# Gathering, adding and normalising both layers' expert results inside the attentions that follow, with all narrow keys and values made in the second routing

## The chip, the cores and the metric

The kernel runs on one core of a Trainium2 chip. The metric is the device time of one execution, in microseconds. Five engines work side by side, each through an instruction list of its own, and meet by semaphores: TensorE (PE), VectorE (DVE), ScalarE (ACT), GpSimd (POOL) and SyncE (SP). SyncE only issues transfers here; GpSimd also issues the indirect ones, which gather or scatter rows by an index tile.

## What is computed

Four layers follow each other on x of 16 batches of 112 tokens, 256 wide, with a context of 375 rows for each batch. Every step is a residual: x = x + f(layernorm(x)). The reference, cut to its last lines and to the two mixtures of experts:

```python
x = x + _L0_xattn_ref(_layernorm(x), ctx, ctx, ...)             # focused linear attention
x = x + _L0_ffn_ref(_layernorm(x), ...)                         # experts, gated
x = x + _L1_xattn_ref(_layernorm(x), ctx, ctx, key_mask, ...)   # tanh attention
x = x + _L1_ffn_ref(_layernorm(x), ...)                         # shared experts
x = x + _L2_xattn_ref(_layernorm(x), ctx, ...)                  # wide softmax, 16 heads of 64
x = x + _L2_ffn_ref(_layernorm(x), ...)                         # experts, normed
x = x + _L3_xattn_ref(_layernorm(x), ctx, ctx, mask, ...)       # narrow softmax, 16 heads of 16
x = x + _L3_ffn_ref(_layernorm(x), ...)                         # ternary

# _L0_ffn_ref, the end: each token takes two expert rows, weighted
ys = yb[jnp.minimum(slot, E * C - 1)] * (weights * kept)[:, None]
out = jnp.zeros((T, D), x.dtype).at[tokens].add(ys)

# _L2_ffn_ref, the end: the same sum, the tokens added, and a layer norm of its own
out = out.reshape(b, s, h) + hidden_states
return _layernorm(out, ln_w, ln_b)
```

## The kernel before

Everything is float32. x stays on the chip as one tile, 112 partitions by 16 batches by 256; nearly every loop runs over the 16 batches. The program is a row of stages, each a block of instruction lists for the five engines; a stage begins when all engines have finished the one before. Inside a stage the lists are written out by hand, and what waits for what is a `wait_ge` on a semaphore; `c.link` and `c.step` (class Chain) make an instruction of VectorE wait for the one before it.

The stages: `focused_attention`, then `routed_experts` for layer 0 (`route`, `run_experts`, `combine`), `tanh_attention`, `shared_experts`, `softmax_attention` wide (L2_xattn), `routed_experts` for layer 2, `softmax_attention` narrow (L3_xattn), `ternary_ffn`. Both layers' expert stages share their code, and the trace drops digits from names: `L_ffnr_`, `L_ffne_` and `L_ffnc_` are route, experts and combine of either layer, `L_xattn_` is either softmax attention.

**route** norms the tokens, computes the experts' logits, picks two for each token, and works out by a running count (`cum`, two matmuls) to which slot each row goes. The weights need an exponential (L2388, ScalarE). GpSimd then issues 32 indirect stores (L2364, 16 batches by 2 choices) that scatter rows to `xbuf` in memory. For layer 2 the stage also prepares the ternary weights of the last stage (`tw.prepare`, `tw.sum`).

**Keys and values beside it.** The contexts' projections are work for TensorE that depends on nothing, so they are put beside the expert stages in parts. Each part is some matmuls into one of two PSUM banks (`project`) and one ScalarE copy out of it (`take`). For layer 0 it is the wide attention's keys and values (`SpilledKeysValues`, 14 parts for a batch), which are stored to memory by SyncE: batches 0 to 3 in the focused attention, 4 to 6 in route, 7 in combine. For layer 2 it is the narrow ones (`KeysValues`, 4 parts for a batch, kept on the chip): batches 0 to 9 in route, 10 to 15 in combine. In `route` the parts stand in three lists: BESIDE (16, one beside each batch's logits), AHEAD (8, ahead of the count and of the exponential) and BEHIND (the rest).

**combine** (L2745 on) has GpSimd gather two expert rows for each token (L2787, `got`, a ring of 4 batches). VectorE adds them with their weights `r.p` (L2812, L2814) and takes the statistics of the sum (L2817, L2818). In layer 0 this is all, and the sum goes into x. In layer 2 it goes into `r.xf`; a square root over all 16 batches (L2799) and a norm of six VectorE instructions for each batch (L2827 to L2833) follow, the last two of which take the statistics of the new x.

**tanh_attention** computes scores, tanh and exponential in 6 chunks for each batch, 96 in all. VectorE norms x one batch ahead (L697), GpSimd makes the block-diagonal queries (`qbd`, L648) and the values with a column of ones (`vaug`), ScalarE does nothing but tanh (L679) and exponential (L671).

**softmax_attention, narrow**: for each batch and head TensorE computes scores (L1375). VectorE adds the mask into `ssb` and takes the minimum (L1230), ScalarE takes the exponential into a ring `p` of 8 (L1165), TensorE turns it (L1387), VectorE copies three of four turned heads out (L1241), ScalarE the fourth, and TensorE multiplies with the values (L1410). The residual of the batch before (L1265, L1268, L101 to L104) stands at head pair 14 of a body, the norm of the batch after next (L1214) at pair 12. The loops over batches of the other engines than TensorE are hardware loops here and in the tanh attention (`each_batch`: the first and last two bodies stand alone, the middle is a loop of two).

The lines of `combine` that take the results:

```python
c.link(dve.scalar_tensor_tensor(out=half[:, h, :], in0=got[:, b % RING, 0, :], scalar=r.p[:, 0, b:b + 1],
                                in1=to, op0=ALU.mult, op1=ALU.add))
dve.scalar_tensor_tensor(out=to, in0=got[:, b % RING, 1, :], scalar=r.p[:, 1, b:b + 1],
                         in1=half[:, h, :], op0=ALU.mult, op1=ALU.add).then_inc(summed, 1)
```

## Time and profile before

| | us |
|---|---|
| median of 3 runs (lowest to highest) | 2900.87 (2896.5 to 2906.04) |
| the profiled execution, its own time | 2931.14 |
| its span | 2929.4 |
| combine of layer 0 (833.3 to 902.3) | 69.0 |
| combine of layer 2 (2296.9 to 2392.2) | 95.3 |
| last attention from its first exponentials on (2408 to 2760) | 352 |
| mean granted TensorE clock | 0.935 of full speed |

A row of a timeline is the start in us, the duration, the engine, the line and operation, the tiles written and read, and in brackets how long the engine was idle ahead of it and what released it. "issue" means that the trace shows nothing it waited for. PEld, the loading of weights, runs beside PE. All times of rows belong to the one profiled execution, and starts are counted from the start of its span.

### The profile page before, as it was taken

How to read it: one execution, taken by the hardware profiler on the slowest of the kernel's cores; microseconds unless marked ns; L12 is line 12 of the kernel's file. 1: busy time of each engine (PE TensorE's matmuls, PEld its weight loads, DVE VectorE, ACT ScalarE, POOL GpSimd, SP SyncE). 2: the span in 40 equal slices, each digit the busy share in tenths (PEclk: the TensorE clock that was granted, in tenths of full speed). 3: DMA queues.
4: the chain of work that ended last, by engine and by line, in shares of the span. 5: the costliest groups of instructions: out<-in, count | busy, mean ns of one | idle time of the engine just before them, and what ended most of it. 6: DMA issues, size and time to landing. Idle time of an engine off the chain costs nothing. (4 is left out here: it accounts for less than half of the span.)

```text
span 2929.4 us, 47164 instructions
## 1 busy us (share of the span) xinstructions
PE 2512.4 (86%) x15874; PEld 1754.4 (60%) x15874; DVE 1372.3 (47%) x4867; ACT 1130.7 (39%) x2617; POOL 797.8 (27%) x867
## 2 busy tenths in 40 slices
PE   6999749999956998979999999883999559999786
PEld 4676428888832554647666565562999336666544
DVE  6988512222232654546643333442111367777665
ACT  4555211111105991234443434331333126666431
POOL 3443140000041210027754444404000401221242
PEclk8999879999977998989999999996999779999898
DMA  4222352222023210043310000044888310000000
GB/s 138 82 101 102 133 197 108 93 84 94 24 85 118 67 54 1 1 134 133 113 36 6 11 6 6 1 155 172 322 325 325 127 35 11 8 11 6 1 7 19
DMA packets 69939, 252.57 MB, mean 86 GB/s; under 512 B 16395, under 2 KB 32040, under 8 KB 52264
## 3 DMA queue, kind: packets, MB, share of 16 engines
q1 hardware_dynamic: 60008, 226.24, 22.2%
q0 software_dynamic: 9744, 23.87, 2.6%
q8 instruction: 114, 1.87, 0.3%
q14 instruction: 73, 0.60, 0.1%
HBM read 197.97 MB, written 52.10 MB: 85 GB/s over the span
## 5 line engine op out<-in xcount | busy, mean ns | idle before, releaser
L2732 PE MATMUL L_ffne_up<-L_ffne_xT,L_ffne_wu 128*128 128x128 f32 (+1 forms) x2144 | 389.8, 337 | 7.3 <-DMA L_ffne_wu<-in_L_ffn_up 7.3
L2732 PEld LDWEIGHTS L_ffne_up<-L_ffne_xT,L_ffne_wu 128*128 128x128 f32 x2144 | 328.1, 193 | 54.3 <-DMA L_ffne_wu<-in_L_ffn_up 6.9
L1082 POOL TENSOR_SCALAR L_xattn_p<-L_xattn_p,L_xattn_rec 112x375 f32<-112x375 f32 x256 | 311.8, 1225 | 0.0
L1387 PEld LDWEIGHTS L_xattn_pt<-ident,L_xattn_p 112*125 112x125 f32 x1536 | 197.3, 189 | 166.4 <-ACT L_xattn_p L1165 75.7
L2717 PE MATMUL L_ffne_dn<-L_ffne_wd,L_ffne_hT 128*112 128x256 f32 (+1 forms) x1200 | 266.3, 379 | 1.5 <-issue 1.5
L1387 PE MATMUL L_xattn_pt<-ident,L_xattn_p 112*125 112x112 f32 x1536 | 247.3, 289 | 20.5 <-DVE L_xattn_pt L1241 16.0
L1224 DVE TENSOR_REDUCE L_xattn_least<-L_xattn_s 112x1 f32<-112x375 f32 x256 | 128.4, 543 | 284.7 <-PE L_xattn_s L1375 284.4
L2717 PEld LDWEIGHTS L_ffne_dn<-L_ffne_wd,L_ffne_hT 128*112 128x112 f32 (+1 forms) x1200 | 216.8, 183 | 39.7 <-issue 2.1
L1241 DVE COPY L_xattn_pt<-L_xattn_pt 125x336 f32<-125x336 f32 x448 | 210.6, 497 | 52.6 <-PE L_xattn_pt L1387 52.4
L1165 ACT ACTIVATE L_xattn_p<-L_xattn_s,L_xattn_least 112x375 f32<-112x375 f32 x256 | 145.1, 570 | 186.2 <-DVE L_xattn_least L1224 186.1
L2620 POOL DMA_DIRECT2D L_ffn_ybuf<-L_ffne_y x75 | 40.1, 534 | 641.3 <-DVE L_ffne_y L2670 386.8
L1165 ACT ACTIVATE L_xattn_p<-L_xattn_ssb,L_xattn_least 112x375 f32<-112x375 f32 x256 | 153.8, 602 | 129.9 <-DVE L_xattn_least L1230 129.0
L2642 ACT ACTIVATE L_ffne_sg<-L_ffne_up 128x280 f32<-128x280 f32 x128 | 51.6, 403 | 329.0 <-PE L_ffne_up L2732 329.0
L2644 ACT ACTIVATE L_ffne_hT<-L_ffne_up,L_ffne_b 128x128 f32<-128x128 f32 x280 | 98.9, 366 | 154.9 <-DMA L_ffne_b<-in_L_ffn_b 76.0
L1230 DVE CUSTOM_DVE_ANT_0 L_xattn_ssb<-L_xattn_s,L_xattn_hide 112x375 f32<-112x375 f32 x256 | 130.8, 545 | 57.4 <-issue 37.7
L1080 POOL TENSOR_TENSOR pool_tick<-ident 1x1 f32<-1x1 f32 x128 | 23.4, 183 | 478.7 <-DVE L_xattn_rec L1236 478.7
L1410 PE MATMUL L_xattn_o<-L_xattn_pt,L_xattn_v 125*64 125x112 f32 (+1 forms) x3072 | 153.4, 268 | 0.0
L2688 DVE TENSOR_TENSOR L_ffne_hT<-L_ffne_sg,L_ffne_up 128x280 f32<-128x280 f32 x128 | 57.1, 446 | 189.2 <-ACT L_ffne_sg L2642 189.2
L1410 PEld LDWEIGHTS L_xattn_o<-L_xattn_pt,L_xattn_v 125*64 125x64 f32 (+1 forms) x3072 | 110.1, 118 | 45.8 <-issue 26.2
L1375 PE MATMUL L_xattn_s<-L_xattn_kt,L_xattn_qt 64*112 64x375 f32 x512 | 116.4, 532 | 17.7 <-ACT L_xattn_p L1165 17.7
L671 ACT ACTIVATE ta_pT<-ta_pT,ta_hide_b,ta_cap 125x896 f32<-125x896 f32 x96 | 121.8, 1272 | 0.0
L1375 PE MATMUL L_xattn_s<-L_xattn_kt,L_xattn_qbd 64*112 64x375 f32 x512 | 115.3, 528 | 2.7 <-POOL L_xattn_qbd L1093 2.7
(369 smaller groups left out, 4480.0 us busy)
## 6 DMA issues: line engine op xcount, KB each, us to landing
L_ffne_wd<-in_L_ffn_down SPq DMA_DIRECT2D x43, 1024.0 KB, 4.9
L_ffne_wu<-in_L_ffn_up SPq DMA_DIRECT2D x35, 1024.0 KB, 5.2
L_ffne_wu<-in_L_ffn_up SPq DMA_DIRECT2D x8, 2048.0 KB, 7.9
L_xattn_kt<-L_xattn_kd SPq DMA_DIRECT2D x8, 1500.0 KB, 7.9
L_xattn_v<-L_xattn_vd SPq DMA_DIRECT2D x8, 1500.0 KB
L_ffn_xbuf<-L_ffnr_zeros SPq DMA_DIRECT2D x8, 1120.0 KB, 12.7
fa_ctxT<-in_ctxT SPq DMA_DIRECT2D x16, 375.0 KB, 3.6
fa_rows<-in_ctx_rows SPq DMA_DIRECT2D x16, 375.0 KB
```

Source lines behind the costliest of these rows:

```text
L671: act.activation(p, p, ACT.Exp, bias=hide_b[:, h, c % KT:c % KT + 1], scale=cap[0:KP, :]).then_inc(exp_done, 1)
L1082: p = pool.tensor_scalar(p_sb[:, head % RP, :], p_sb[:, head % RP, :], rec[:, h, head:head + 1], None, ALU.mult)
L1165: act.activation(p_sb[:, head % RP, :], src, ACT.Exp, bias=least[:, h, head:head + 1], scale=-1.0, accum_out=sums[:, h, head:head + 1]).th ...
L1224: dve.tensor_reduce(low, s, AX.X, ALU.min).then_inc(low_done, 1)
L1230: dve.tensor_tensor_reduce(out=ssb[:, head % 4, :], in0=s, in1=hide[:, h, :], scale=1.0, scalar=3e38, op0=ALU.add, op1=ALU.min, accum_out= ...
L1241: dve.tensor_copy(pt_sb[:, head % RP, :, :], pt_ps[head % 2][0:KP, 0, 0:KT * S].rearrange("p (k s) -> p k s", k=KT)).then_inc(pt_done, 1)
L1375: m = pe.matmul(score_ps(b, n)[0:S, 0, 0:SK], q, k, start=True, stop=True)
L1387: m = pe.transpose(pt_ps[head % 2][0:KP, 0, kt * S:(kt + 1) * S], p_sb[:, head % RP, kt * KP:(kt + 1) * KP], ident[0:S, 0:S])
L1410: m = pe.matmul(o_ps[n * VC:n * VC + dh, chunk // 4, chunk % 4 * S:(chunk % 4 + 1) * S], v, pt_sb[:, (head + n) % RP, kt, :], start=(kt == ...
L2644: act.activation(hT[:, h, f, q * RH:(q + 1) * RH], src, ACT.Gelu, bias=b1[:, h, f:f + 1]).then_inc(h_done, 1)
L2717: m = pe.matmul(dn_ps[i][0:TR, 0, 0:D], hT[:, h, f, t * TR:(t + 1) * TR], wd[:, h, f, :], start=(f == 0), stop=(f == FC - 1))
L2732: m = pe.matmul(up_ps[s % RING][k][:, 0, 0:RH], wu[:, h, c, k * FF + f * 128:k * FF + (f + 1) * 128], xT[:, h, c, q * RH:(q + 1) * RH], st ...
```

## The change

There is no combine stage any more. `routed_experts` calls the following attention itself and hands it the routing `r`.

- *Layer 0.* `tanh_attention` gathers into a ring of four batches. The first four are gathered and added in its opening, ahead of the norm of batch 0; batches 4 + 2b and 5 + 2b are gathered and added at the end of body b, for b from 0 to 5. The square roots of x's variances come in three groups: batches 0 to 3 in the opening, 4 to 7 at body 2 and 8 to 15 at body 6, between chunks of tanh and exponential.
- *Layer 2.* The narrow attention gathers into a ring of three, six batches in the opening and one for each body behind. VectorE adds batches 0 and 1 and norms them ahead of its first two `xn`; batches 2 and 3 are added behind those, and the other 12 additions and 14 norms stand in the bodies (`beside`). The norm is two `scalar_tensor_tensor` and the statistics; beta has been added to x in `route` (16 additions behind the slots), gamma is `ln_w`. ScalarE takes the roots for two batches at a time, at head 8 of every even body up to 12.
- *Room for it.* The masked scores are written where the exponentials will stand: `ssb` is gone, `p` has 6 heads, and VectorE waits for the turning of six heads before, not for an exponential. `onT` is `o_sb`, and the mask is single.
- *Keys and values.* The wide ones of batch 7 and all narrow ones are made in the routings. AHEAD has four parts, `tw.sum` stands behind 12 parts of BEHIND, which has 44 for layer 2. A batch's values are stored in three pieces. The stores are waited for at the end of `run_experts` instead of the end of each stage.
- *Loops.* The hardware loops of both attentions are unrolled.

The diff, cut to its core:

```diff
@@ tanh_attention @@
+                for b in range(OPENING):
+                    gather(b)
...
                     pool.tensor_copy(vaug[:, h, :, :, 0:DH],
                                      ctxr[:, h, :, :].rearrange("p k (h d) -> p k h d", h=H)).then_inc(v_done, 1)
-                each_batch(pool, body)
+                    for later in arriving(b):
+                        gather(later)
...
+                        if c == 2 and b in (2, 6):
+                            deviations(1 if b == 2 else 2)
...
+                    for later in arriving(b):
+                        add_experts(later)
+                for b in range(OPENING):
+                    add_experts(b)
                 normalize(0, 0)
@@ softmax_attention @@
+                        if not wide and head == 8 and b % 2 == 0 and b + 2 < NB:
+                            root(b // 2 + 1)
+                            if b + 4 < NB:
+                                root_of_sums(b // 2 + 2)
...
+                def add_normed(b):
+                    n, to = b // 2, r.xf[:, b, :]
+                    if b == 0:
+                        dve.wait_ge(ln_in, 16)
+                    if b % 2 == 0:
+                        dve.wait_ge(root_done, n + 1)
+                        ch.link(dve.reciprocal(rstd3[:, b:b + 2], std3[:, b:b + 2]))
+                    ch.link(dve.scalar_tensor_tensor(out=to, in0=to, scalar=core.mv2[:, b, 0:1], in1=ln_w[:, :],
+                                                     op0=ALU.subtract, op1=ALU.mult))
+                    ch.link(dve.scalar_tensor_tensor(out=x[:, b, :], in0=to, scalar=rstd3[:, b:b + 1], in1=x[:, b, :],
+                                                     op0=ALU.mult, op1=ALU.add))
+                    ch.link(dve.bn_stats(core.st46[:, 2 + b % 2, :], x[:, b, :]))
+                    ch.link(dve.bn_aggr(core.mv[:, b, :], core.st46[:, 2 + b % 2, :]))
+                    if b % 2:
+                        dve.sem_inc(stats_done, 1)
+                def beside(b, pair):
+                    if pair == 0 and b == 0:
+                        add_experts(4)
+                    if pair == 2 and 5 + b < NB:
+                        add_experts(5 + b)
+                    if b == 0 and pair in (4, 6):
+                        add_normed(pair // 2)
+                    if b % 2 == 0 and pair == 14 and b + 4 < NB:
+                        add_normed(b + 4)
+                    if b % 2 == 1 and pair == 6 and b + 4 < NB:
+                        add_normed(b + 4)
...
-                        after(dve, exp_done, b * H + head - 3)
+                        after(dve, t_out, b * H + head - PP + 1)
                         dve.memset(core.tick[:, head:head + 1], 0.0)
-                        dve.tensor_tensor_reduce(out=ssb[:, head % 4, :], in0=s, in1=hide[:, h, :], scale=1.0,
+                        dve.tensor_tensor_reduce(out=at_p(b, head), in0=s, in1=hide[:, h, :], scale=1.0,
@@ KeysValues, route, run_experts @@
-        self.spans = {"r_": (0, 10), "c_": (10, NB)}
+        self.spans = {"r_": (0, NB)}
...
-        BESIDE, AHEAD = parts[0:NB], parts[NB:NB + 8]
-        BEHIND = parts[NB + 8:]
+        BESIDE, AHEAD = parts[0:NB], parts[NB:NB + 4]
+        BEHIND = parts[NB + 4:]
...
                 dve.wait_ge(slots_done, 1)
+                if not twice:
+                    for b in range(NB):
+                        c.step(dve.tensor_tensor(x[:, b, :], x[:, b, :], after_b[:, :], ALU.add))
                 if tw:
                     tw.prepare(dve, lg_ps[0])
...
-                    if tw and n == len(BEHIND) - 4:
+                    if tw and n == 12:
                         tw.sum(pe, lg_ps[0])
...
                 each_block(sp, N, body)
+                if spilled:
+                    spilled.wait_stored(sp)
```

TensorE's list in the routing of layer 2, around the two matmuls of the count (`L_ffnr_cum`); `L_xattnkvr_ps` written from `wk` and `wv` are the keys and values of one batch, and `tw_wsum` is the sum of the ternary weights. Before:

```order
L2521 MATMUL L_ffnr_lg<-L_ffnr_wr,L_ffnr_xt 112x8 x2
L2117 MATMUL L_xattnkvr_ps<-L_xattnkvr_ctxT,L_xattnkvr_wk 128x375 x4
L2122 MATMUL L_xattnkvr_ps<-L_xattnkvr_wv,L_xattnkvr_ctxT 125x256 x6
L2117 MATMUL L_xattnkvr_ps<-L_xattnkvr_ctxT,L_xattnkvr_wk 128x375 x4
L2122 MATMUL L_xattnkvr_ps<-L_xattnkvr_wv,L_xattnkvr_ctxT 125x256 x6
L2540 MATMUL L_ffnr_cum<-L_ffnr_picked,L_ffnr_before 112x128
L2541 MATMUL L_ffnr_cum<-L_ffnr_picked,L_ffnr_ones 112x128
L2117 MATMUL L_xattnkvr_ps<-L_xattnkvr_ctxT,L_xattnkvr_wk 128x375 x4
L2122 MATMUL L_xattnkvr_ps<-L_xattnkvr_wv,L_xattnkvr_ctxT 125x256 x6
L2117 MATMUL L_xattnkvr_ps<-L_xattnkvr_ctxT,L_xattnkvr_wk 128x375 x4
L2122 MATMUL L_xattnkvr_ps<-L_xattnkvr_wv,L_xattnkvr_ctxT 125x256 x6
L2117 MATMUL L_xattnkvr_ps<-L_xattnkvr_ctxT,L_xattnkvr_wk 128x375 x4
```

and now:

```order
L2672 MATMUL L_ffnr_lg<-L_ffnr_wr,L_ffnr_xt 112x8 x2
L2259 MATMUL L_xattnkvr_ps<-L_xattnkvr_ctxT,L_xattnkvr_wk 128x375 x4
L2264 MATMUL L_xattnkvr_ps<-L_xattnkvr_wv,L_xattnkvr_ctxT 125x256 x6
L2691 MATMUL L_ffnr_cum<-L_ffnr_picked,L_ffnr_before 112x128
L2692 MATMUL L_ffnr_cum<-L_ffnr_picked,L_ffnr_ones 112x128
L2259 MATMUL L_xattnkvr_ps<-L_xattnkvr_ctxT,L_xattnkvr_wk 128x375 x4
L2264 MATMUL L_xattnkvr_ps<-L_xattnkvr_wv,L_xattnkvr_ctxT 125x256 x6
L2259 MATMUL L_xattnkvr_ps<-L_xattnkvr_ctxT,L_xattnkvr_wk 128x375 x4
L2264 MATMUL L_xattnkvr_ps<-L_xattnkvr_wv,L_xattnkvr_ctxT 125x256 x6
L2259 MATMUL L_xattnkvr_ps<-L_xattnkvr_ctxT,L_xattnkvr_wk 128x375 x4
L2264 MATMUL L_xattnkvr_ps<-L_xattnkvr_wv,L_xattnkvr_ctxT 125x256 x6
L1861 MATMUL L_ffnr_lg<-tw_wsum,tw_ones 128x2
```

One batch of parts (two of these rows) less stands ahead of the count. The ternary sum stands behind three batches of parts in both; one more batch follows it before, eight now.

VectorE's list at the opening of the last attention, from about the addition of the bias (`L_xattn_bias_y`) on. Before:

```order
L1205 MEMSET L_xattn_o 128x512
L1207 TENSOR_TENSOR L_xattn_bias_y<-L_xattn_s,L_xattn_bias_y 112x256
L1214 TENSOR_SCALAR L_xattn_xn<-x_sb,mv,rstd 112x256 x2
L1229 MEMSET tick 1x1
L1230 ISA L_xattn_ssb,L_xattn_least<-L_xattn_s,L_xattn_hide 112x375
L1230 ISA L_xattn_least 112x1
```

and now, up to the first instructions of the norm of batch 0:

```order
L1298 TENSOR_TENSOR L_xattn_bias_y<-L_xattn_s,L_xattn_bias_y 112x256
L1305 SCALAR_TENSOR_TENSOR L_xattn_got<-L_xattn_got,L_ffn_p,L_ffn_xf 112x256
L1307 SCALAR_TENSOR_TENSOR L_ffn_xf<-L_xattn_got,L_ffn_p 112x256
L1310 BN_STATS st<-L_ffn_xf 112x6
L1311 BN_AGGR mv<-st 112x2
L1305 SCALAR_TENSOR_TENSOR L_xattn_got<-L_xattn_got,L_ffn_p,L_ffn_xf 112x256
L1307 SCALAR_TENSOR_TENSOR L_ffn_xf<-L_xattn_got,L_ffn_p 112x256
L1310 BN_STATS st<-L_ffn_xf 112x6
L1311 BN_AGGR mv<-st 112x2
L1322 RECIPROCAL L_xattn_rstd<-L_xattn_std 112x2
L1323 SCALAR_TENSOR_TENSOR L_ffn_xf<-L_ffn_xf,mv,L_xattn_ln_w 112x256
L1325 SCALAR_TENSOR_TENSOR x_sb<-L_ffn_xf,L_xattn_rstd,x_sb 112x256
```

The two `xn` follow the bias directly before; now the first two batches' additions (L1305 to L1311) and norms (L1323 to L1328) stand between.

VectorE's list in the last attention at head pair 14 of an even body, around the residual of the batch before (`xs`). Before:

```order
L1230 ISA L_xattn_ssb,L_xattn_least<-L_xattn_s,L_xattn_hide 112x375
L1230 ISA L_xattn_least 112x1
L1241 COPY L_xattn_pt<-L_xattn_pt 125x336
L1265 TENSOR_TENSOR xs<-L_xattn_s,L_xattn_bias_y 112x256
L1268 TENSOR_TENSOR xs<-xs,x_sb 112x256
L101 BN_STATS st<-xs 112x6
L102 TENSOR_SCALAR x_sb<-xs 112x256
L103 BN_AGGR mv<-st 112x2
L104 TENSOR_SCALAR mv<-mv 112x2
```

and now:

```order
L1378 COPY L_xattn_pt<-L_xattn_pt 125x336
L1402 TENSOR_TENSOR xs<-L_xattn_s,L_xattn_bias_y 112x256
L1405 TENSOR_TENSOR xs<-xs,x_sb 112x256
L102 BN_STATS st<-xs 112x6
L103 TENSOR_SCALAR x_sb<-xs 112x256
L104 BN_AGGR mv<-st 112x2
L105 TENSOR_SCALAR mv<-mv 112x2
L1322 RECIPROCAL L_xattn_rstd<-L_xattn_std 112x2
L1323 SCALAR_TENSOR_TENSOR L_ffn_xf<-L_ffn_xf,mv,L_xattn_ln_w 112x256
L1325 SCALAR_TENSOR_TENSOR x_sb<-L_ffn_xf,L_xattn_rstd,x_sb 112x256
L1327 BN_STATS st<-x_sb 112x6
L1328 BN_AGGR mv<-st 112x2
```

The norm of a batch four ahead is appended to the residual.

## Rows read from the trace of the kernel before

**Rows 1.** Busy time by engine in five stretches, granted PEclk, DMA share, GB/s
```profile
379.00:426.00 47.00, 17.26 (x47) 8.32 (x45) 0.00 (x0) 6.48 (x12) 30.36 (x32) 0.71 0.54 172
833.30:902.30 69.00, 31.11 (x56) 13.63 (x56) 24.86 (x64) 7.45 (x14) 29.84 (x32) 0.67 0.31 104
2296.90:2392.20 95.30, 40.58 (x120) 25.73 (x120) 59.65 (x162) 14.13 (x26) 30.46 (x32) 0.70 0.24 71
913.00:1097.00 184.00, 175.35 (x2044) 90.66 (x2044) 102.10 (x144) 181.11 (x190) 42.52 (x62) 0.99 0.24 78
2408.00:2760.00 352.00, 328.09 (x3222) 219.96 (x3222) 258.07 (x1105) 208.54 (x654) 68.22 (x64) 0.98 0.03 8
```

**Rows 2.** Timeline, ScalarE, combine of layer 0: start, duration, idle before and releaser
```profile
855.18 0.48 ACT L2245 ACTIVATE L_xattnkvc_ks<-L_xattnkvc_ps 128x375 f32<-128x375 f32 x1 [6.61 <-remote]
...
876.91 0.60 ACT L2248 ACTIVATE L_xattnkvc_vs<-L_xattnkvc_ps 125x512 f32<-125x512 f32 x1 [10.71 <-remote]
```

**Rows 3.** Timeline, ScalarE, combine of layer 2
```profile
2317.62 0.38 ACT L2137 ACTIVATE L_xattn_v<-L_xattnkvc_ps 125x256 f32<-125x256 f32 x1 [6.54 <-DMA L_xattnkvctxT<-in_ctxT]
...
2337.32 0.57 ACT L2135 ACTIVATE L_xattn_kt<-L_xattnkvc_ps,L_xattnkvc_bk 128x375 f32<-128x375 f32 x1 [10.66 <-issue]
...
2351.17 0.38 ACT L2137 ACTIVATE L_xattn_v<-L_xattnkvc_ps 125x256 f32<-125x256 f32 x1 [0.27 <-PE L_xattnkvc_ps L2122]
2351.57 1.28 ACT L2799 ACT_TABLE_LOAD   x1
2352.87 0.31 ACT L2799 ACTIVATE L_ffnc_std<-mv,L_ffnc_tiny 112x16 f32<-112x16 f32 x1
```

**Rows 4.** Groups by line, GpSimd, combine of layer 0: the gathers
```profile
L2787 POOL DMA_INDIRECT L_ffnc_got<-L_ffn_ybuf,L_ffn_get x32 | 29.8, 933 | 16.1 <-issue 15.5 <-DVE x_sb L2814 0.6
```

**Rows 5.** Timeline, VectorE, combine of layer 0: fourth batch added
```profile
846.30 0.48 DVE L2812 SCALAR_TENSOR_TENSOR L_ffnc_half<-L_ffnc_got,L_ffn_p,x_sb 112x256 f32<-112x256 f32 x1 [1.45 <-DMA L_ffnc_got<-L_ffn_ybuf,L_ffn_get]
...
847.80 0.18 DVE L2818 BATCH_NORM_AGGREGATE mv<-st 112x2 f32<-112x6 f32 x1
```

**Rows 6.** Timeline, VectorE and TensorE, opening of the tanh attention
```profile
904.24 0.41 DVE L697 TENSOR_SCALAR ta_xn<-x_sb,mv,rstd 112x256 f32<-112x256 f32 x1
...
913.50 1.86 PE L760 MATMUL ta_s_ps<-ta_qbd,ta_kT 64*125 64x448 f32 x4 [8.16 <-DMA ta_ctxr<-in_ctx_rows]
```

**Rows 7.** Timeline, VectorE, opening of the last attention
```profile
2401.92 0.42 DVE L1207 TENSOR_TENSOR L_xattn_bias_y<-L_xattn_s,L_xattn_bias_y 112x256 f32<-112x256 f32 x1 [3.17 <-PE L_xattn_s L1441]
2402.38 0.74 DVE L1214 TENSOR_SCALAR L_xattn_xn<-x_sb,mv,rstd 112x256 f32<-112x256 f32 x2
```

**Rows 8.** Waits in the last attention: total us, times, longest
```profile
DVE L_xattn_ssb L1230 <- issue: 37.7, 55, 1.3
...
PE L_xattn_pt L1387 <- DVE L_xattn_pt L1241: 16.0, 16, 1.4
```

**Rows 9.** Timeline, VectorE and TensorE, around one residual of the last attention
```profile
2488.13 0.41 DVE L1265 TENSOR_TENSOR xs<-L_xattn_s,L_xattn_bias_y 112x256 f32<-112x256 f32 x1
...
2490.13 0.17 DVE L104 TENSOR_SCALAR mv<-mv 112x2 f32 x1
...
2492.54 0.75 PE L1387 MATMUL L_xattn_pt<-ident,L_xattn_p 112*125 112x112 f32 x4 [1.36 <-DVE L_xattn_pt L1241]
```

**Rows 10.** Timeline, VectorE and TensorE, routing of layer 0
```profile
370.75 0.17 DVE L2447 TENSOR_SCALAR L_ffn_p<-L_ffnr_gap 112x16 f32<-112x16 f32 x1 [7.82 <-ACT L_ffnr_gap L2388]
...
430.72 0.63 PE L2705 MATMUL L_ffne_t<-ident,L_ffne_rows 112*128 112x112 f32 x2 [34.45 <-DMA L_ffne_rows<-L_ffn_xbuf]
```

**Rows 11.** Timeline, TensorE and GpSimd, routing of layer 2
```profile
1978.61 2.77 PE L2117 MATMUL L_xattnkvr_ps<-L_xattnkvr_ctxT,L_xattnkvr_wk 128*128 128x375 f32 x8
...
1981.22 2.75 PE L2122 MATMUL L_xattnkvr_ps<-L_xattnkvr_wv,L_xattnkvr_ctxT 128*125 128x256 f32 x12
...
1982.30 2.15 POOL L2364 DMA_INDIRECT L_ffn_xbuf<-L_ffn_xf,L_ffn_put  x1 [0.30 <-issue]
...
2026.39 0.69 PE L2705 MATMUL L_ffne_t<-ident,L_ffne_rows 128*128 128x128 f32 x2 [42.41 <-DMA L_ffne_rows<-L_ffn_xbuf]
```

326 lines of the change are left out of this document (170 added, 156 removed).

## The prediction

> **What bounds the kernel now.** I read the busy table by stage first, then the ScalarE timeline of the two combine stages, then the openings of the two attentions that follow them, and last the waits inside the last attention. In the combine of layer 0 no engine is busy for half of its 69.0 us, and in that of layer 2 the busiest, VectorE, has 59.65 of 95.3 [rows 1]: these stages are bound by chains and by their ends, not by work. The stages that are to take the work in look otherwise. The tanh attention is bound by ScalarE (181.11 of 184.0 us), the last attention by TensorE (328.09 of 352.0), with VectorE at 258.07 [rows 1]. GpSimd has room in both (42.52 and 68.22).
>
> Inside the combines ScalarE stands still three times each, up to 10.71 and 10.66 us, and the releaser shown is "remote", "issue" or a load that lies long before [rows 2, 3]. Between the first and the last of them they take 27.4 and 25.3 us. I work out that layer 0's combine would end some 24.5 us earlier without them (its last keys and values, and the store behind them, follow on ScalarE) and layer 2's some 10 us (its square root stands behind half of the parts [rows 3]). That is 34.5 us, and the profiled execution is 2931.14 against a median of 2900.87, 30.3 more. So I take these waits for a thing of the profiled execution. The sum is made in its terms, and the 34.5 us are taken off where it is carried over to the median.
>
> **Layer 0: what goes.** The whole stage, -69.0. Its 32 gathers go to GpSimd inside the tanh attention, at 0.93 us each [rows 4]. Eight stand in the opening, the other 24 in six bodies, four each: 3.7 us of GpSimd in a body of 11.5 (184.0 / 16), where it has 2.7 so far (42.52 / 16 [rows 1]). They hide.
>
> **Opening of the tanh attention.** xn is made 1.9 us after the stage's start (904.24 against 902.3), and the first scores start at +11.2, since they wait for the context rows [rows 6]. Now xn needs four batches added. In the combine the fourth is added from +13.0 to +14.7 (846.30 and 847.80 + 0.18, less 833.3) [rows 5]. Square root and reciprocal bring xn to +15.2, transpose, copy and block diagonal add 3.5, scores at +18.7: +7.5. The opening's own loads are now beside the gathers, +5 more at worst.
>
> **Inside the tanh attention.** ScalarE takes two further square roots. Each is a table load (1.28), the root (0.31) and a table load back (1.28) [rows 3], 2.87 us, on the engine that is the bound: +5.7. VectorE adds 12 batches, 1.68 us each [rows 5], and has 82 us free of 184; it delays a copy now and then, +1.5 (0 to +5). Here the rows speak against a rule. The table load begins 0.02 us after the take ahead of it has ended (2351.17 + 0.38), and the root 0.02 after the load [rows 3]: nothing else is paid. The Trainium skill, ScalarE: Activation LUTs, section "What ACT_TABLE_LOAD costs", adds a drain of some 1.38 us to every switch. By that the two pauses would cost 5.5 us more here, and the seven in the last attention up to 19 more; the trace shows no such drain, and the sum leaves it out.
>
> **Routing of layer 0.** VectorE waits 7.82 us for an exponential that stands on ScalarE behind eight parts of keys and values [rows 10]. Four are now ahead of it. A part takes 1.5 (14 parts are 31.11 us at clock 0.67 [rows 1], 20.8 at full clock), so the scattering begins 6.0 earlier. TensorE gets batch 7's 14 parts, 20.8 us, into a hole of 34.45 [rows 10]; they end with the last scatters. But the stores of batch 7 now run into the experts' first weight loads, where DMA share is already 0.54 [rows 1]. I take -3, between -6 and +5.
>
> **Layer 2: what goes.** The whole stage, -95.3.
>
> **Opening of the last attention.** Today xn follows the bias addition at +10.1 (2401.92 + 0.42, less 2392.2) [rows 7]. Behind that addition there now stand two batches added (2 x 1.68 [rows 5]), a root with its table load (1.6 [rows 3]), a reciprocal and two batches normed (0.3 + 2 x 1.68: two operations of the same form and the same statistics), a second root and reciprocal (0.8): 9.5. GpSimd's sixth gather waits for the third batch's addition, which VectorE makes after both xn; the block diagonal stands behind that gather and is late by 0.5 more. +10 (+8 to +12).
>
> **Inside the last attention.** VectorE gets 12 additions and 14 norms, 26 x 1.68 = 44 us. The row to cost them by is the residual of the batch before: a block from 2488.13 to 2490.30, 2.2 us, after which TensorE waits 1.36 for a copy of VectorE [rows 9]; there are 16 such waits in the stage, 16.0 us together [rows 8]. So TensorE forgives some 0.8 us of a block. 21 blocks that stand alone cost 0.85 each, 18; five that are appended to a residual or stand close behind one cost all of 1.68, 8: together +26. Lower bound: a block alone is forgiven altogether, +10. Upper bound: VectorE is the bound, its 258.07 busy and 37.7 of "issue" gaps [rows 1, 8] fill 296 of 352, with 44 more 340; if VectorE is late in every body, all 44 are paid. ScalarE's seven pauses of 3.0 us (two roots share the loads) stand in an engine with 208.54 of 352 busy; the slack of one is about as long as the pause, +5 (0 to +21). That the masked scores are now written where the exponentials stand makes VectorE wait for TensorE's transposes of six heads before, which are issued ahead of the scores it reads: 0.
>
> **Routing of layer 2.** Four parts fewer ahead of the exponential bring the scattering 5.5 forward (a batch, that is four parts, takes 2.77 + 2.75 [rows 11]). TensorE gets 24 more parts, 33 us, into a hole of 42.41 [rows 11], but now waits for the ternary weights' sum in the midst of them: VectorE first adds beta to 16 batches (16 x 0.42, a sum of that form in rows 7), so some 7 us. 33 + 7 is the hole but 2: the stage ends where it ended, 0 (-2 to +15). The scatters next to VectorE's large operations take 2.15 instead of 0.93 [rows 11, 4], three or four of them, as before.
>
> **Sum.** Layer 0: -69.0 + 7.5 + 5.7 + 1.5 - 3 = -57.3. Layer 2: -95.3 + 10 + 26 + 5 + 0 = -54.3. Together -111.6 in the terms of the profiled execution, 2819.5. With the 34.5 of unexplained waits taken off it is -77.1, and from the median 2824. The two ways meet; I say 2821. Loops that are unrolled on four engines count for nothing.
>
> **The rivals.**
> *A, the waits are real and stay behind* (the median has them as well and the gap of 30.3 us lies elsewhere): all of -112 shows, 2789. For it: nothing in the rows says that a profile makes them. Against: their sum fits the gap.
> *B, the last attention turns VectorE-bound*: 44 for 26, with 16 more of ScalarE's pauses, 2821 + 34 = 2855. For it: 340 of 352 us. Against: TensorE's waits per block are shorter than the block.
> *C, the waits go with the gathers*: they appear in the attentions' openings or in the routings, where 14 and 24 more parts stand; three or four of 8.8 us (52.7 / 6) make 2821 + 30 = 2851.
> *D, slower than before*: the same wait, but once for each body that gathers, of which there are 16 (6 and 10), and twice in the openings: 18 x 8.8 = 158, 2901 - 112 + 158 = 2947. In the tanh attention ScalarE has no slack for any. It decides from 13 such waits on. For it: the waits occur only while gathers run. Against: 64 gathers made six of them. The Trainium skill, SBUF — State Buffer, section "Who interferes with whom", holds that a DMA never contends with a compute engine; by it C and D would fall, and the trace doesn't decide it, since it names no releaser.
> *E, the stages aren't gone*: the openings wait for all gathers (32 x (0.93 + 0.30) [rows 4, 11] = 39 us each). The ring of four lets eight gathers through before the first addition, so no: under 1 in 100.
>
> **How the numbers follow.** Forecast 0.58 (2800 to 2840), A 0.12, B 0.13, C 0.11, D 0.03, and 0.03 for a mix that ends near 2901. The range runs from A to B with the openings' bounds: 2787 to 2859. What a measurement can tell from no change is some 0.3%, 9 us. Faster 0.94, same 0.02, slower 0.04.
>
> **What would show it.** Right: first scores of the tanh attention near +19 and of the last one near +26 after their stages' starts; the last attention longer by 30 us, with TensorE's wait for VectorE's copies up from 16.0 to some 40; ScalarE's pauses of 2.9 us, two and seven; routings that end within 6 us of today's. Wrong: ScalarE waits of 7 to 11 us without a releaser in the attentions or routings (C, D); the last attention longer by 50 or more with VectorE above 85% (B); a profiled execution that still exceeds its median by 30 us (A); TensorE idle for over 10 us in the routing of layer 2, or rows of the experts that come in late behind the stores.

## The result and the profile after

The changed kernel takes 2868.82 us (median of 4, 2862.49 to 2878.91) against 2902.11 for the kernel before beside it: ratio 0.989, interval 0.9856 to 0.9924. It is faster by 33 us where 80 were forecast, and lies above the range of 2787 to 2859. Timed again on another occasion (`after_again` below) the ratio is 0.9892.

The first profile of before (2929.4 us) holds the odd ScalarE waits of [rows 2, 3], and its timed runs evidently don't. A second profile of the same kernel, `before_again`, has a span of 2899.0 us and none of these waits. All comparisons below are made against it, and numbers for which no run is named are those of the changed kernel's first profile. A stretch of the table reaches from the first transfer of one stage to the first of the next, in us:

| stretch | before_again | after | difference | forecast |
|---|---|---|---|---|
| focused attention | 315.9 | 314.9 | -1.0 | 0 |
| route, layer 0 | 113.4 | 115.5 | +2.1 | -3 |
| experts and combine, layer 0 | 457.2 | 426.9 | -30.3 | -44.5 |
| tanh attention, shared experts | 372.1 | 396.7 | +24.6 | +14.7 |
| wide attention | 630.5 | 635.1 | +4.6 | 0 |
| route, layer 2 | 118.9 | 121.6 | +2.7 | 0 |
| experts and combine, layer 2 | 356.0 | 271.6 | -84.4 | -85.3 |
| last attention, ternary | 535.0 | 578.5 | +43.5 | +41 |
| sum | 2899.0 | 2860.8 | -38.2 | -77.1 |

The forecast column has the 34.5 us of odd waits taken off where they stood (24.5 and 10). So the combines are gone as forecast; three places gave back more. Here are the busy times by stretch, cut at whole us (start:end, length, busy time and number of instructions of PE, PEld, DVE, ACT and POOL, granted clock, DMA share, GB/s), of before_again:

```profile
429.00:837.00 408.00, 392.69 (x1744) 316.51 (x1744) 86.52 (x208) 53.00 (x129) 21.09 (x40) 0.98 0.24 85
837.00:886.00 49.00, 23.56 (x56) 11.91 (x56) 24.68 (x64) 7.46 (x14) 30.05 (x32) 0.71 0.44 146
886.00:1259.00 373.00, 331.35 (x2618) 185.62 (x2618) 193.37 (x352) 225.35 (x264) 46.32 (x67) 0.95 0.13 43
...
2280.00:2364.00 84.00, 37.35 (x120) 25.40 (x120) 60.01 (x161) 14.14 (x26) 30.32 (x32) 0.70 0.27 81
2364.00:2899.00 535.00, 453.73 (x3736) 292.13 (x3736) 364.11 (x1308) 254.15 (x742) 126.82 (x105) 0.95 0.04 11
```

and of the changed kernel:

```profile
430.00:857.00 427.00, 391.89 (x1744) 316.02 (x1744) 86.53 (x208) 52.90 (x129) 21.08 (x40) 0.96 0.25 86
857.00:1254.00 397.00, 334.45 (x2618) 186.88 (x2618) 217.27 (x417) 231.75 (x269) 77.81 (x99) 0.94 0.16 50
...
2282.00:2861.00 579.00, 463.88 (x3736) 298.27 (x3736) 421.55 (x1452) 274.44 (x772) 159.44 (x137) 0.93 0.06 17
```

The combines, 49.6 and 84.9 us long (second and fourth row), have no counterpart. The experts of layer 0 take 426.9 us for what took 407.6, with TensorE busy for the same 392; the attentions are longer while TensorE's own work hardly changed, 331.35 before against 334.45 now in the first, and 453.73 against 463.88 in the last.

**Experts of layer 0: +19.3.** SyncE's queue in the changed kernel (start, time that the issue took, line, tiles), and TensorE's first work in the stage, which answers to the second of [rows 10]:

```profile
412.57 2.88 SPq L2337 DMA_DIRECT2D L_xattn_kd<-L_xattnkvks  x1
416.12 12.95 SPq L2342 DMA_DIRECT2D L_xattn_vd<-L_xattnkvvs  x3
430.41 4.31 SPq L2751 DMA_DIRECT2D L_ffne_rows<-L_ffn_xbuf  x1
```

```profile
452.80 2.88 PE L2858 MATMUL L_ffne_t<-ident,L_ffne_rows 112*128 112x112 f32 x10 [30.48 <-DMA L_ffne_rows<-L_ffn_xbuf]
```

Batch 7's keys and its three pieces of values stand on the queue right ahead of the experts' first rows, whose issue alone takes 4.31 us, and 0.34 in before_again. TensorE begins 22.4 us after the stage's start, against 4.8 in before_again (434.02 less 429.27): 17.6 us later. In six more profiles of kernels that leave the store there it begins 19.7 to 27.4 us after.

**Opening of the tanh attention: +10.8.** VectorE's first addition and `xn`, the normed x of batch 0, then TensorE's first scores, which answer to [rows 6]:

```profile
866.70 0.48 DVE L723 SCALAR_TENSOR_TENSOR ta_half<-ta_got,L_ffn_p,x_sb 112x256 f32<-112x256 f32 x1 [16.04 <-DMA ta_got<-L_ffn_ybuf,L_ffn_get]
...
875.70 0.41 DVE L743 TENSOR_SCALAR ta_xn<-x_sb,mv,rstd 112x256 f32<-112x256 f32 x1
```

```profile
879.38 3.35 PE L808 MATMUL ta_s_ps<-ta_qbd,ta_kT 64*125 64x448 f32 x8 [2.58 <-POOL ta_qbd L664]
```

The stage starts at 857.35. The first addition is at +9.35, `xn` at +18.35, scores at +22.0; before_again has scores at +11.2.

**Bodies of the tanh attention: +15.** A body is the part of an engine's list for one batch. From the first tanh to the last exponential there are 184.8 us in before_again and 199.8 here. A body of 11.49 us is bound by ScalarE; the third to eighth take 15.29, 11.49, 13.52, 13.75, 18.31 and 11.77, and all after them 11.49. In a 13.8 us body ScalarE waits, and VectorE's list has hardly a hole that isn't a round trip to TensorE, that is, a wait for TensorE's answer to what VectorE has just handed it:

```profile
935.19 0.42 DVE L766 TENSOR_TENSOR xs<-ta_fin_ps,x_sb 112x256 f32<-112x256 f32 x1 [1.34 <-PE ta_fin_ps L836]
...
937.46 0.62 DVE L755 COPY ta_o_sb<-ta_o_ps 128x448 f32<-128x448 f32 x1 [0.76 <-PE ta_o_ps L823]
939.33 2.96 DVE L760 RECIPROCAL ta_rz<-ta_fin_ps 128x448 f32<-128x448 f32 x1 [1.25 <-PE ta_fin_ps L831]
...
942.87 0.48 DVE L723 SCALAR_TENSOR_TENSOR ta_half<-ta_got,L_ffn_p,x_sb 112x256 f32<-112x256 f32 x1
...
946.30 0.41 DVE L743 TENSOR_SCALAR ta_xn<-x_sb,mv,rstd 112x256 f32<-112x256 f32 x1
...
948.95 0.42 DVE L766 TENSOR_TENSOR xs<-ta_fin_ps,x_sb 112x256 f32<-112x256 f32 x1 [1.34 <-PE ta_fin_ps L836]
```

From residual to residual it is 13.76 us. Each wait in brackets is the answer of TensorE to the instruction ahead of it on VectorE. The two new additions with their statistics (942.87 to 946.30, 3.4 us) stand between the division and the next `xn`, on which TensorE's next scores depend. The two pauses of ScalarE (a table load, a root, a table load back) are as forecast, 2.9 us each:

```profile
967.34 1.28 ACT L683 ACT_TABLE_LOAD   x1
968.63 0.30 ACT L683 ACTIVATE std<-mv,eps 112x8 f32<-112x8 f32 x1
968.95 1.28 ACT L703 ACT_TABLE_LOAD   x1
970.24 1.01 ACT L703 ACTIVATE ta_pT<-ta_s_ps,ta_tscale 125x896 f32<-125x896 f32 x1
```

**Last attention: +43.5.** Opening, answering to [rows 7]: the bias addition at +11.4 of the stage's start, 2282.32, `xn` at +21.3, scores at +27.9.

```profile
2293.72 0.42 DVE L1298 TENSOR_TENSOR L_xattn_bias_y<-L_xattn_s,L_xattn_bias_y 112x256 f32<-112x256 f32 x1 [2.85 <-PE L_xattn_s L1583]
...
2303.66 0.73 DVE L1351 TENSOR_SCALAR L_xattn_xn<-x_sb,mv,rstd 112x256 f32<-112x256 f32 x2
```

```profile
2310.22 1.59 PE L1517 MATMUL L_xattn_s<-L_xattn_kt,L_xattn_qbd 64*112 64x375 f32 x4 [2.67 <-POOL L_xattn_qbd L1159]
```

Scores began at +17.1 in before_again: +10.8. From there to the last output are 377.0 us, and 343.7 in before_again; this is what "the stretch" of the last attention means below. Here it is for the changed kernel, with TensorE's waits for VectorE's copies (total us, times, longest), answering to [rows 8]:

```profile
2310.22:2687.21 376.99, 336.38 (x3222) 223.81 (x3222) 303.61 (x1214) 225.75 (x679) 88.49 (x82) 0.96 0.05 14
...
PE L_xattn_pt L1529 <- DVE L_xattn_pt L1378: 34.7, 36, 3.0
```

and of before_again:

```profile
2381.00:2725.00 344.00, 325.33 (x3222) 217.49 (x3222) 255.69 (x1097) 207.16 (x652) 67.33 (x63) 0.99 0.03 8
...
PE L_xattn_pt L1387 <- DVE L_xattn_pt L1241: 16.0, 16, 1.3
```

Of 33.3 us, 18.7 are waits for VectorE's copies (34.7 less 16.0), 3.3 waits for ScalarE's copies, and 11.1 are the same 3222 matmuls at a granted clock of 0.96 instead of 0.99 of full speed (336.38 against 325.33 busy). The granted clock is a mean over times at 2.4 GHz and times at 1.2. At 1.2 GHz TensorE stands for 27.3 us of this stretch, and for 5.1 in before_again; half of the difference is the 11.1. Of the 27.3, 3.4 us follow on from the opening, 10.2 are in the first body, around a wait of 2.96 us for VectorE, and 13.7 stand right behind two of the five waits of 2.35 us and more that come later. One of those two, in rows of the stretch:

```profile
2402.00:2433.10 31.10, 27.11 (x281) 17.50 (x279) 25.25 (x102) 18.22 (x54) 6.35 (x6) 1.00 0.06 14
2433.10:2439.90 6.80, 6.58 (x32) 5.13 (x36) 5.74 (x22) 3.96 (x14) 3.07 (x4) 0.50 0.13 36
```

The wait ends at 2433.32.

### The profile page after: what moved, and what is told of

Its sections match the earlier page's. It is cut to its first block and busy times, and to the rows that moved or that the text cites. A ratio compares the mean times of both kernels' runs of the same rounds, so it can differ in the third digit from the quotient of the medians.

```text
span 2860.8 us, 46447 instructions
## 1 busy us (share of the span) xinstructions
PE 2514.2 (88%) x15874; PEld 1758.3 (61%) x15874; DVE 1373.1 (48%) x4867; ACT 1156.6 (40%) x2651; POOL 801.7 (28%) x867
## 5 line engine op out<-in xcount | busy, mean ns | idle before, releaser
L1529 PE MATMUL L_xattn_pt<-ident,L_xattn_p 112*125 112x112 f32 x1536 | 251.0, 292 | 42.7 <-DVE L_xattn_pt L1378 34.7
L1249 ACT ACTIVATE L_xattn_p<-L_xattn_p,L_xattn_least 112x375 f32<-112x375 f32 x256 | 153.7, 601 | 142.9 <-DVE L_xattn_least L1367 142.5
L1367 DVE CUSTOM_DVE_ANT_0 L_xattn_p<-L_xattn_s,L_xattn_hide 112x375 f32<-112x375 f32 x256 | 131.0, 545 | 36.1 <-issue 31.5
L1517 PE MATMUL L_xattn_s<-L_xattn_kt,L_xattn_qt 64*112 64x375 f32 x512 | 117.2, 535 | 17.1 <-ACT L_xattn_p L1249 17.0
L695 ACT ACTIVATE ta_pT<-ta_pT,ta_hide_b,ta_cap 125x896 f32<-125x896 f32 x96 | 113.1, 1181 | 0.0
## 6 DMA issues: line engine op xcount, KB each, us to landing
L_ffn_xbuf<-L_ffnr_zeros SPq DMA_DIRECT2D x8, 1120.0 KB, 13.7
```

The costliest lines, as they stand in the source:

```text
L695: act.activation(p, p, ACT.Exp, bias=hide_b[:, h, c % KT:c % KT + 1], scale=cap[0:KP, :]).then_inc(exp_done, 1)
L1249: act.activation(at_p(b, head), src, ACT.Exp, bias=least[:, h, head:head + 1], scale=-1.0, accum_out=sums[:, h, head:head + 1]).then_inc(e ...
L1367: dve.tensor_tensor_reduce(out=at_p(b, head), in0=s, in1=hide[:, h, :], scale=1.0, scalar=3e38, op0=ALU.add, op1=ALU.min, accum_out=low).t ...
L1517: m = pe.matmul(score_ps(b, n)[0:S, 0, 0:SK], q, k, start=True, stop=True)
L1529: m = pe.transpose(pt_ps[head % 2][0:KP, 0, kt * S:(kt + 1) * S], at_p(b, head)[:, kt * KP:(kt + 1) * KP], ident[0:S, 0:S])
```

## The experiments

Each ratio is to the kernel before on the same chip. `before_again` is that kernel under a new label.

> The kernel before, once more, for a second profile. Theory 1 (the ScalarE waits of 7 to 11 us without a cause in the two combine stages belong to profiled executions and are not in the timed ones): they are in this profile again, six of them, some 50 us together, and the profiled execution is 25 to 35 us above the timed ones. Theory 2 (they are in every execution): they are there, and the profiled execution is within 8 us of the timed ones. Theory 3 (an accident of the first profile): they are gone or elsewhere, combine stages 45 and 85 us long, profiled and timed executions agree.

Measured 2903.22 us, ratio 1.0012 (1.0000 to 1.0023), span 2899.0. The odd waits are absent, and the combines take 49.6 and 84.9 us instead of 69.0 and 95.3: the third theory.

**One layer at a time.** `l0_only` keeps the change's layer 0 and before's `combine` for layer 2, `l2_only` the other way round:

```diff
 # l0_only
-            softmax_attention(core, "L3_xattn", keys=keys, r=r)
+            combine(core, pre, r, True, keys)
...
+                softmax_attention(core, "L3_xattn", keys=keys)
 # l2_only
-                tanh_attention(core, r, sw)
+            combine(core, pre, r, False, keys)
...
+            tanh_attention(core, sw)
```

> The layer 0 half of the change alone (gathering in the tanh attention, batch 7's keys and values in the routing); layer 2 as before. Theory 1: the stage that goes is worth 69.0 - 24.5 = 44.5 us of time, and the changed kernel's trace shows it given back: experts 20 later behind the stores, tanh attention with its opening 26 longer. Sum 0, 2895 to 2908. Theory 2 (the waits were real): 24 us faster than before, about 2878. The forecast would have it 33 faster, 2869.

> The layer 2 half alone (gathering, adding and norming in the last attention, all narrow keys and values in the second routing); layer 0 as before. Theory 1: 95.3 - 10 us go, 41 come back in the last attention, 2 in the routing: 42 us faster, 2855 to 2866. Theory 2: 52 us faster, 2850. The forecast would have it 44 faster, 2858.

Measured: `l0_only` 2900.52 us, ratio 0.9993 (0.998 to 1.0006), no gain at all; `l2_only` 2864.17 us, 0.9872 (0.9852 to 0.9892), the whole gain. The last attention's stretch is 346.5 us in the first and 377.3 in the second; the tanh stretch, from the first tanh to the last exponential, is 199.3 and 184.8. The two halves don't act on each other.

**Where the store stands.** In `late_store` batch 7's last stores are issued behind the experts' second round of loads; in `wait_back` SyncE waits for all stores at the end of `route`, as before.

```diff
 # late_store
+            if b + 1 < self.end:
                 self.store_values(sp, b)
...
+                    if spilled and isinstance(b, int) and b == 1:
+                        spilled.store_last(sp)
 # wait_back
+        self.wait_stored(sp)
```

> The changed kernel, with the stores of batch 7's wide keys and values issued on SyncE's queue behind the experts' loads for the first two experts, instead of ahead of them. Theory (the queue is in order, and the experts' first rows stand behind 3 MB of stores): TensorE starts the experts within 6 us of the stage's start instead of 22, the kernel is 15 to 20 us faster than the changed one, about 2851. Rival (the loads are slow because transfers of any kind share the 16 DMA engines, or because the scatters are late): less than 5 us, 2864 to 2870, and the rows still come 15 us or more after the stage's start.

> The changed kernel, but the stores of the wide keys and values are waited for at the end of the routing again. Theory (the experts' first loads stand behind the stores on SyncE's queue in any case): the stage starts some 20 us later, the first rows come when they came, within 4 us of the changed kernel, 2866 to 2874. Rival (moving the wait let part of the loads pass the stores): 10 us or more slower, 2879 or more.

`late_store`: 2847.29 us, ratio 0.9805 (0.9781 to 0.9829). SyncE and TensorE in it:

```profile
428.27 0.34 SPq L2759 DMA_DIRECT2D L_ffne_rows<-L_ffn_xbuf  x1
...
431.36 2.44 SPq L2355 DMA_DIRECT2D L_xattn_kd<-L_xattnkvks  x1
433.84 13.73 SPq L2357 DMA_DIRECT2D L_xattn_vd<-L_xattnkvvs  x3
```

```profile
433.56 2.87 PE L2868 MATMUL L_ffne_t<-ident,L_ffne_rows 112*128 112x112 f32 x10 [15.04 <-DMA L_ffne_rows<-L_ffn_xbuf]
```

The same 3 MB are now issued 19 us later, behind the first loads and beside the experts' work, and TensorE begins 5.3 us after the stage's start instead of 22.4. With that the layer 0 half of the change is worth something: 0.9805 against the 0.9872 of `l2_only`. The stage takes 408.8 us, before_again's 407.6, so the traffic itself costs hardly anything; its place ahead of the first loads did. Nor were the DMA engines full while TensorE waited in the changed kernel (the last two numbers are the DMA share and GB/s):

```profile
430.40:440.00 9.60, 0.00 (x0) 0.00 (x0) 0.00 (x0) 1.28 (x1) 0.00 (x0) 0.50 0.46 157
```

In `late_store` the share is 0.79 over the first 5.4 us. `wait_back`: 2897.84 us, 0.9865 (0.9839 to 0.9891). Its experts start at 457.86 and TensorE 4.9 us later: the wait has moved, not gone. It was timed on another chip than `late_store`, whose routings are longer (see the last section); there TensorE begins 10.8 us after the stage's start with the store in its place, and `late_store`'s edit is worth less (0.9842 against 0.9873 below).

**VectorE's additions in the tanh attention.** Four edits. `tanh_adds` makes them one body later, between residual and the take of o; `late_adds` is that with the late store; `late_gap` has them between the take and the reciprocal, where VectorE waits 1.25 us for TensorE anyway, with the late store; in `narrow` they are left out but for 8 of 256 columns (batches 4 to 15 here, 6 to 15 in the last attention). The take is VectorE's copy of the weighted sums out of PSUM (L755). The first three also move ScalarE's two pauses, from chunk 2 to chunk 4 of their bodies.

```diff
 # tanh_adds, late_adds, late_gap
-                        if c == 2 and b in (2, 6):
+                        if c == 4 and b in (2, 6):
 # tanh_adds, late_adds
+                    if b > 0:
+                        for later in arriving(b - 1):
+                            add_experts(later)
                     if b > 0:
                         take_o(b - 1, 1 - h)
 # late_gap
                         take_o(b - 1, 1 - h)
+                        for later in arriving(b - 1):
+                            add_experts(later)
                         divide(b - 1, ch)
-                    for later in arriving(b):
-                        add_experts(later)
 # narrow
+                    w = D if b < OPENING else 8
-                    ... got[:, b % RING, 0, :] ...
+                    ... got[:, b % RING, 0, 0:w] ...
```

> The changed kernel, with VectorE's additions of two batches in the tanh attention made one body later and behind the copy of the turned x, not at the body's end ahead of the next norm (and the two square roots at chunk 4 instead of 2). Theory (at the body's end they lengthen the chain from one batch's division over the next norm, transpose and block diagonal to the scores, and ScalarE stands 7.9 us in bodies 3 to 6): ScalarE's waits for scores go to under 2 us, 7 us faster than the changed kernel, about 2862. Rival (VectorE simply has too much to do, or the gathers come late): no change, 2869, the waits move to another body.

> Both edits: the stores of batch 7 behind the experts' first loads, and the tanh attention's additions one body later. Theory: 21.5 + 7, 2840. Rival (each only moves the loss): 2847.

> The changed kernel with two edits: batch 7's wide keys and values are stored behind the experts' first loads (as in late_store, worth 0.86% of the time there), and in the tanh attention the scaled adds of a batch are moved from behind the reciprocal, where they are a part of VectorE's serial chain, into its wait for ScalarE's spread of the sums, one body later. Theory that VectorE's chain sets these six bodies: the chain goes from 13.8 to about 12.6 us, so six bodies give some 7 us back, the tanh stage from 200 to about 192 us, and the kernel comes to about 0.978 of before. Theory that ScalarE's own work and its table loads set them: the stage stays at 199 to 200 us, and the ratio at 0.980 as for late_store.

> The changed kernel with the two scaled adds and the statistics of the later batches cut to 8 of 256 columns: batches 4 to 15 in the tanh attention, batches 6 to 15 in the last attention. Left out is the rest of these sums; gathers, roots, waits and all other work stay. Tanh attention, theory that VectorE's adds lengthen the bodies: a body's chain falls from 13.8 to about 11.3 us, under ScalarE's 11.5, only the two pauses for roots are left, and the stretch from first tanh to last exponential goes from 200 to 188 to 191 us. Theory that the gathers or the pauses do it: it stays within 2 us of 200. Last attention, theory that the blocks of adds stop TensorE: the stretch from first scores to last output goes from 377 to about 368 us (ten times 0.85); theory that the normed sums in front of and behind the residual do it: it stays above 374.

`tanh_adds` 2897.13 us, 0.9873 (0.9843 to 0.9903), `late_adds` 2886.14, 0.9842 (0.9821 to 0.9863). Both have a longer stretch, 207.1 and 207.5 us, where 7 us less was expected: there the additions stand between TensorE's answer and the take of o, still in the chain. The pauses' new place isn't the reason, since `late_gap` shares it. `late_gap`: 2841.64 us, 0.9804 (0.9779 to 0.9828). The bodies with additions and without a pause take 12.72 to 12.85 us, near the 12.6 of its theory, because the additions now lie in the round trip:

```profile
915.44 0.42 DVE L766 TENSOR_TENSOR xs<-ta_fin_ps,x_sb 112x256 f32<-112x256 f32 x1 [1.34 <-PE ta_fin_ps L836]
...
917.71 0.62 DVE L755 COPY ta_o_sb<-ta_o_ps 128x448 f32<-128x448 f32 x1 [0.76 <-PE ta_o_ps L823]
918.25 0.79 DVE L723 SCALAR_TENSOR_TENSOR ta_half<-ta_got,L_ffn_p,x_sb 112x256 f32<-112x256 f32 x1
...
922.00 2.96 DVE L760 RECIPROCAL ta_rz<-ta_fin_ps 128x448 f32<-128x448 f32 x1
...
928.17 0.42 DVE L766 TENSOR_TENSOR xs<-ta_fin_ps,x_sb 112x256 f32<-112x256 f32 x1 [1.34 <-PE ta_fin_ps L836]
```

But the stretch is 197.8 us, not 192 as its theory had it. In the changed kernel a pause of ScalarE was partly hidden by VectorE's chain (15.29 and 11.49 together are 2 x 13.4); with the chain at 12.7 the two bodies with pauses take 14.74 and 15.77. The changed kernel's code of this stage gives 198.8 to 203.6 in seven other profiles, and that of `late_gap` 197.7 to 197.8 in three, so the edit is worth about 3 us, too little to time. `narrow`: 2861.3 us, 0.9862 (0.9847 to 0.9877), stretch 193.6 us, between the two theories. Of its 8.8 us over 184.8 the two pauses are 5.8; the 3 left are bodies of 11.8 to 12.2 us, whose chain still holds 1.9 us of short additions and statistics. So of the 15 us the columns left out are 5 to 10, and the gathers on GpSimd, which `narrow` keeps, nothing that shows.

**No table loads.** `no_roots` leaves out ScalarE's later square roots, in the tanh attention as here and in the last attention likewise, and so their table loads.

```diff
-                    act.activation(core.std[:, span], mv[:, span, 1], ACT.Sqrt,
+                    act.activation(core.std[:, span], mv[:, span, 1], ACT.Identity if n else ACT.Sqrt,
```

> The changed kernel with ScalarE's later square roots (two in the tanh attention, seven pairs in the last attention) replaced by an identity, which needs no table load; the standard deviations of those batches are left out, variance plus epsilon stands in their place. Theory (a pause costs two loads of 1.28 and is half hidden in the last attention): 5.7 + 5 = 11 us faster, 2858. Rival 1 (no slack in the last attention): 5.7 + 21 = 27, 2842. Rival 2 (all of the last attention's loss is VectorE's): 6, 2863.

2884.24 us, 0.9831 (0.981 to 0.9851), on the chip of `wait_back` (0.9865), whose interval overlaps. The tanh stretch is 201.4 us, and 201.5 in `wait_back` with roots, with six bodies of 13.2 to 15.6 instead of two long ones: while VectorE's chain is as it is, the pauses are free behind it. In the last attention the stretch is 376.5 against 377.0, but that doesn't say that the seven pauses cost nothing. TensorE is idle for 34.4 us of it, and for 37.1 to 42.4 in eight profiles with the same last attention and its roots; but its clock is 0.94, with five falls to 1.2 GHz behind TensorE's long waits, where the changed kernel's 377.0 us have two. So the pauses cost some 3 to 8 us of waits, and the lower clock took them back in this one execution.

**What stops TensorE in the last attention.** `pool_sum` gives ten batches' additions to GpSimd; `norm_pair` takes the normed sum from behind the residual (heads 14, 15) to heads 10, 11; `spread` cuts every new block in two and puts the halves at different heads; `narrow`, above, leaves most of the additions' work out.

```diff
 # pool_sum
+                    pc.link(pool.tensor_scalar(y0, y0, r.p[:, 0, b:b + 1], None, ALU.mult))
+                    pc.link(pool.tensor_scalar(y1, y1, r.p[:, 1, b:b + 1], None, ALU.mult))
+                    pc.link(pool.tensor_tensor(y0, y0, y1, ALU.add))
+                    pool.tensor_tensor(to, to, y0, ALU.add).then_inc(psummed, 1)
 # norm_pair
-                    if b % 2 == 0 and pair == 14 and b + 4 < NB:
+                    if b % 2 == 0 and pair == 10 and b + 4 < NB:
 # spread
+                        if pair == 2:
+                            add_experts(5 + b)
+                        if pair == 4:
+                            measure_sum(5 + b)
...
+                        if pair == (6 if b % 2 else 10):
+                            add_normed(b + 4)
+                        if pair == (10 if b % 2 else 12):
+                            measure_x(b + 4)
```

The changed kernel, timed beside `pool_sum` and `late_gap`:

> The changed kernel itself, timed again beside the kernel before on the chip of the three runs that follow. If the change is worth what its own timing gave, the ratio is 0.989 within its interval, and the ratios of the single parts read on other chips can be set against it. If the odd 7 to 11 us waits of ScalarE belong to the chip, they stand in this profile exactly when they stand in those of the other kernels of this chip.

> The changed kernel, but in the last attention GpSimd adds the experts' rows for batches 6 to 15 (four operations each, in place of VectorE's two of 0.85 us), and VectorE only takes the statistics of the norm. Theory that VectorE's blocks between the evictions are what TensorE waits for in the even bodies: ten blocks shrink by 1.7 us to less than TensorE forgives, so the stretch from first scores to last output goes from 377 to about 365 us, ratio about 0.986. Rival: GpSimd's operations slow VectorE's beside them, or the gathers now come late behind them, and the stretch stays at 377 us or grows. If it was never the blocks but the lower granted clock of this stage (0.96), it stays at 377 too.

> The changed kernel, but in the even bodies of the last attention the normed sum of batch b+4 (1.93 us of VectorE) stands at heads 10 and 11 instead of behind the residual (1.96 us) at heads 14 and 15. Theory that TensorE stops for the pile of both (3.9 us, wait 2.35 us, six times): the wait falls to the residual's own 1.36 us, the second block costs 0.5 to 1.1 us of its own, so 0 to 3 us less; ratio 0.988 to 0.989. If the pile is what lowers the clock, the stretch goes from 377 to about 365 us.

> The changed kernel with all of VectorE's new work in the last attention cut into pieces of at most 1.7 us: scaled adds at head 2, their statistics at head 4; normed sum at head 10 (even bodies) or 6 (odd), its statistics at head 12 or 10. No work is taken away. Theory that the size of the blocks between two copies for TensorE sets the cost: TensorE's waits for VectorE go from 34.7 to under 20 us, the granted clock from 0.96 to 0.98, and the stretch from 377 to about 355 us; ratio near 0.981. Theory that it is the sum of VectorE's work (48 us more than before over 344): the waits only move, and the stretch stays at 374 to 380 us.

`after_again` 2870.06 us, 0.9892 (0.986 to 0.9925). `pool_sum` 2870.42, 0.9887 (0.9857 to 0.9918), no gain: VectorE is busy for 11 us less in the stretch and TensorE waits for it as long (31.9 us, and 31.9 in after_again). One reason may be in VectorE's row, beside GpSimd's at that moment (two of the 38 such operations in the stage are like it):

```profile
2443.08 2.61 DVE L1343 SCALAR_TENSOR_TENSOR x_sb<-L_ffn_xf,L_xattn_rstd,x_sb 112x256 f32<-112x256 f32 x1
```

```profile
2442.85 0.79 POOL L1165 TENSOR_TENSOR L_ffn_xf<-L_ffn_xf,L_xattn_got 112x256 f32<-112x256 f32 x1
2443.59 1.82 POOL L1173 TENSOR_TENSOR L_xattn_qbd<-L_xattn_qt,halfmask 128x448 f32<-128x448 f32 x2
```

An operation that takes 0.48 us elsewhere in this attention takes 2.61. The changed kernel has a smaller case of it in ten of its bodies: the addition's second `scalar_tensor_tensor` stands beside a GpSimd operation and takes 1.14 us.

```profile
2435.46 1.14 DVE L1307 SCALAR_TENSOR_TENSOR L_ffn_xf<-L_xattn_got,L_ffn_p 112x256 f32<-112x256 f32 x1
```

```profile
2435.20 1.12 POOL L1173 TENSOR_TENSOR L_xattn_rec_w<-L_xattn_rec,one 112x512 f32<-112x512 f32 x1 [16.48 <-DVE L_xattn_rec L1373]
```

An addition with its statistics is thus 2.25 us there (2435.03 to 2437.28), not the 1.68 of the forecast. `narrow` takes the additions away without giving GpSimd anything, and its stretch is 379.1 us, its waits:

```profile
PE L_xattn_pt L1531 <- DVE L_xattn_pt L1380: 28.3, 31, 3.1
```

In the two profiles of the changed kernel they are 34.7 and 31.9 us. So the additions, which stand alone, stop TensorE for 4 to 6 us in all. The long waits are seen in the changed kernel at the end of even bodies, VectorE and TensorE:

```profile
2427.91 0.41 DVE L1402 TENSOR_TENSOR xs<-L_xattn_s,L_xattn_bias_y 112x256 f32<-112x256 f32 x1
...
2432.67 0.08 DVE L1367 DVE_READ_ACCUMULATOR2_ANT L_xattn_least<- 112x1 f32 x1
```

```profile
2426.42 0.91 PE L1529 MATMUL L_xattn_pt<-ident,L_xattn_p 112*125 112x112 f32 x6
...
2433.32 1.57 PE L1529 MATMUL L_xattn_pt<-ident,L_xattn_p 112*125 112x112 f32 x6 [2.35 <-DVE L_xattn_pt L1378]
```

The residual of batch b-1 begins at 2427.91, the reciprocal (2429.77) and the normed sum of b+4 follow to 2431.65, two masked minima stand ahead of the next copy, and TensorE waits 2.35 us. Behind the wait six matmuls of the same form take 1.57 us instead of 0.91: that is the clock's fall shown above. There are five such piles of a residual and a normed sum, with waits of 2.35 to 2.45 us. `norm_pair` takes this pile apart: 2855.7 us, 0.9833 (0.9818 to 0.9848), stretch 366.6 us.

```profile
2314.00:2680.00 366.00, 332.01 (x3222) 220.54 (x3221) 304.44 (x1214) 225.64 (x679) 88.58 (x82) 0.98 0.06 15
...
PE L_xattn_pt L1529 <- DVE L_xattn_pt L1378: 27.3, 39, 3.1
```

Waits are down by 7.4 us, and TensorE is busy for some 4 us less at a clock of 0.98. The waits of 2.35 us and more are gone; behind the first body none is longer than 0.98 us. The 365 us that were expected if the pile lowers the clock came out, and the timed ratio is clear of the changed kernel's 0.989 too. `spread`, with the same work in smaller pieces: 2841.19 us, 0.9779 (0.9761 to 0.9798), stretch 358.4 us.

```profile
2311.00:2669.00 358.00, 336.70 (x3222) 223.29 (x3222) 302.49 (x1214) 225.54 (x679) 88.13 (x82) 0.97 0.06 15
...
PE L_xattn_pt L1542 <- DVE L_xattn_pt L1388: 14.8, 22, 3.1
```

TensorE's wait for VectorE is 14.8 us, less than the kernel before had, with VectorE busy for 302.49 us of 358 instead of 255.69 of 344. The sum of VectorE's work was not the bound, the length of a piece was. Of the 33.3 us, 18.6 are back and 14.7 are left: 11.4 of them are TensorE's longer busy time (336.70), at a granted clock of 0.97.

All profiles together tell when the clock falls. Take the stretch without its first 25 and its last 20 us. In the twelve profiles of kernels with piles the clock falls to 1.2 GHz 46 times there, each time from 0.7 us ahead to 2.1 us behind the end of one of the 65 waits of 2.35 us and more. In the six profiles without such waits (before twice, `l0_only`, `norm_pair`, `spread`, `gap_spread`) it falls four times, for 14 us in all; the 46 falls come to 277 us. `spread` and `gap_spread` have none, so the edits that take the long waits away take the falls away with them. What `spread` has left lies at the two ends: 13.2 us at 1.2 GHz behind the longer opening and a wait of 3.10 us in the first body, and 10.2 us in the last body, where the fall comes inside the stretch and not just behind it as in the changed kernel. Why it comes earlier there is open.

**Together.** `best` is late store, gap and `pool_sum`; `gap_spread` is late store, gap and `spread`.

> All three edits in one kernel: late store, the adds of the tanh attention in the gap, GpSimd adding batches 6 to 15 in the last attention. If their gains add, 0.989 less 0.9% less 0.25% less 0.3%, so about 0.975 of before. If the late store is the only one that does anything, 0.980.

> Late store, the adds of the tanh attention in the gap, and VectorE's work of the last attention in small pieces. If small pieces are worth 20 us, 0.974 of before; if they are worth nothing, 0.980 as late_gap.

`best` 2846.58 us, 0.9803 (0.978 to 0.9826): only the late store shows. Its last stretch is 391.7 us at a clock of 0.92, with eight of the long waits and eight falls behind them. `gap_spread` 2822.55 us, 0.9726 (0.9712 to 0.9739), better than before by 80 us and than the changed kernel, timed on other occasions, by some 46. Its last stretch is 358.6 us, its TensorE starts the experts 5.2 us after the stage's start, its tanh stretch is 197.7 us.

## Why the prediction was wrong

Faster was right, the size was not: 33 us instead of 80. Three steps failed: the stores ahead of the experts' loads were priced as traffic (19.3 us), VectorE's free time in the tanh attention was taken for room (15 us where 7.2 were forecast), and TensorE's clock had no term in the last attention (11 us, which other terms happened to make up for). Step by step, in the order of the prediction:

- **The waits taken off.** Right for the chips on which it was timed, in the main: the combines take 49.6 and 84.9 us there, 19.4 and 10.4 less than in the first profile, where 24.5 and 10 were worked out. Rival A (2789) needed them to stay with the timed runs, and falls.
- **Opening of the tanh attention, +7.5.** Mis-sized: +10.8. The fourth batch is added at +17.7, not +14.7. The gathers now run beside the opening's own loads, which was named with +5 more at worst; that these loads are the reason fits, but no run tells it apart.
- **Inside the tanh attention, +5.7 + 1.5.** The pauses are 2.9 us each, as said. The failed term is the 1.5 for VectorE, taken from "has 82 us free of 184". VectorE's free time there is round trips to TensorE, which can't be filled from the end of its list: the additions stood in a chain of 13.8 us against ScalarE's 11.5. +15 in place of +7.2. The upper bound of 5 for VectorE's delay was too low as well, since the additions lengthen the stretch by 5 to 10 us or more.
- **Routing of layer 0, -3.** The step that failed most. It named the stores of batch 7 beside the experts' loads, but priced the traffic, at +5 at worst, and not its place ahead of the loads on one queue: TensorE begins 17.6 us later within the stage than before, which makes +19.3 there, and the routing itself has +2.1 where -3 was said. `late_store` gives this back. That rows of the experts may come late behind the stores stood among the signs of being wrong.
- **Opening of the last attention, +10.** Right: +10.8.
- **Inside the last attention, +26 + 5.** The sum is right, +33.3, the shares are not. The pauses' +5 isn't contradicted: `no_roots` has 3 to 8 us fewer waits. Of VectorE's blocks, the five piled behind a residual cost 2.1 us each (the 10.4 us that `norm_pair` gives back: 1.5 of waits and the rest clock), more than the 1.68 of the sum. The 21 others come to some 11 us of waits (18.7 less 7.4), 0.5 each and not 0.85, though ten of them are longer than was reckoned (2.25 us). And 11 us of the 33 are TensorE's clock, for which the sum had no term: that it came out at 31 is luck.
- **Routing of layer 2, 0.** +2.7, inside its bounds. The first matmul on the expert rows comes after 4.17 us of idle time where it was 42.41 [rows 11]: the hole is filled, as worked out.
- **Wide attention.** No term; +4.6, at clock 0.97 in place of 0.98. In `after_again` it takes 631.6 us, against 630.5 in before_again, so most of this belongs to one execution.
- **Unrolled loops, nothing.** Right in the tanh attention: its bodies without new work take 11.49 us as before.
- **Rivals.** B's sign, the last attention longer by 50 and VectorE above 85%, isn't there. C's waits are there on one chip of three, in the routings, as the last section shows; the changed kernel itself wasn't timed on it. D and E fell. A and B together had 0.25, C 0.11; that the order on one queue alone takes 20 us was no rival.
- **The table-load rule.** The rows of the pause show a load of 1.28, a root 0.01 after it, a load and a tanh 0.01 after that. The drain of 1.38 us that the Trainium skill, ScalarE: Activation LUTs, section "What ACT_TABLE_LOAD costs", adds to every switch isn't there in the changed kernel either.

## What to carry to other kernels

Before work is moved next to an engine that has time free, look at what its free time is made of: holes that are round trips of one chain can't take work at the chain's end, but they can take it inside the round trip. Work between two deliveries for the engine that bounds a stage was priced here by the length of a piece, not by the sum, so cut it and keep it away from pieces that are there already. A long piece costs twice, since TensorE's clock falls behind a long wait. Loads that the next stage begins with go ahead of stores on the same queue. And two stretches of equal length don't show that an edit is free: compare TensorE's idle time and its clock one by one.

## What the runs showed of the hardware

The odd ScalarE waits of [rows 2, 3] go with the chip. On one chip the kernel before takes 2933.85 us, on two others 2900.24 to 2902.78. All four profiles of that chip have such waits and none of the twelve of the other two; there kernels without `combine` have them in the routings, beside the scatters. The record doesn't name the chip of the first profile of before. ScalarE in `late_adds` there:

```profile
404.81 0.60 ACT L2403 ACTIVATE L_xattnkvvs<-L_xattnkvr_ps 125x512 f32<-125x512 f32 x1 [7.09 <-remote]
416.02 0.60 ACT L2403 ACTIVATE L_xattnkvvs<-L_xattnkvr_ps 125x512 f32<-125x512 f32 x1 [10.62 <-issue]
```

Its routings take 133.8 and 137.9 us, where the changed kernel's take 115.5 and 121.6. What releases ScalarE the trace doesn't show. Such waits were seen only in stages with GpSimd's indirect transfers, and not in the attentions, which have some too; whether these hold ScalarE up is not settled, and so the section of the Trainium skill that the prediction set against C, SBUF — State Buffer, "Who interferes with whom", is neither borne out nor refuted.

TensorE's granted clock falls from 2.4 to 1.2 GHz behind single waits of 2.35 us and more in work that is otherwise dense, as the 46 falls above show, but not behind every one: two of five in the first profile of the changed kernel (clock 0.96, stretch 377.0 us), three of five in `after_again` (0.94, 381.5 us). So differences of 5 us in single profiles of this stretch carry nothing; the waits (34.7 and 31.9 us) do better.

A VectorE operation of 112x256 that takes 0.48 us took 2.61 us beside three of GpSimd's element-wise ones in a row, in `pool_sum`, and 1.14 us beside one of 1.12 us, ten times in the changed kernel. Moving such work to GpSimd saved VectorE 11 us in its list and the kernel nothing.
